# Experts of an attention and mixture-of-experts layer: plain scatters in place of adding scatters

## What is computed

```
x = x + cross_attention(layernorm(x), ctx)     # per token: 16 heads by 16 heads, softmax
n = layernorm(x)
shared = (silu(n @ sfc1.T) * (n @ sfc2.T)) @ sfc3.T
top_w, top_idx = top_k(n @ gate_w.T, 2);  top_w = softmax(top_w)
moe = sum over the 2 choices: top_w * ( silu(n @ w1[e].T) @ w2[e].T ),  e = top_idx
x = x + moe + shared
```

## Time and profile before

| | |
|---|---|
| median of 3 runs (lowest, highest) | 1812.68 us (1810.61, 1815.49) |
| the profiled execution, its own time | 1811.71 us |
| its span, first to last instruction | 1809.8 us |
| mean granted TensorE clock | 0.932 of full speed |
| PE, VectorE, ScalarE, GpSimd busy | 1490.7, 1250.5, 774.2, 1276.1 us |
| DMA bytes | 302.36 MB, mean 167 GB/s |

### The profile page before, as it was taken

One profiled execution on the slowest core, in us unless ns is written; L12 is line 12 of the kernel. 1 busy time (PEld: TensorE's weight loads), 2 busy tenths in 40 slices (PEclk: granted clock), 3 DMA queues, 4 the chain that ended last, 5 costly groups with the idle time before them and its releaser, 6 DMA issues.

```text
span 1809.8 us, 49252 instructions
## 1 busy us (share of the span) xinstructions
PE 1490.7 (82%) x17109; PEld 1315.5 (73%) x17110; DVE 1250.5 (69%) x3232; ACT 774.2 (43%) x1490; POOL 1276.1 (71%) x975
## 2 busy tenths in 40 slices
PE   5499999999999999999999999979776676676660
PEld 4477888888888888888888887758666665666650
DVE  7588888888888788888888887876434444334440
ACT  3244445445444444454455444425433333333330
POOL 5266666767676667666766766557888888888887
PEclk9699999999999999999999999999888889888885
DMA  8788888999898889888989988738777776777773
GB/s 195 136 212 184 171 174 209 197 178 192 209 183 179 192 194 188 180 192 211 180 174 210 201 174 185 178 137 213 136 130 134 134 133 108 132 132 134 134 113 36
DMA packets 929510, 302.36 MB, mean 167 GB/s; under 512 B 820882, under 2 KB 891160, under 8 KB 924480
## 3 DMA queue, kind: packets, MB, share of 16 engines
q1 hardware_dynamic: 859920, 178.50, 51.3%
q0 software_dynamic: 54432, 71.81, 21.7%
q10 hardware_dynamic: 15120, 51.57, 8.3%
HBM read 162.62 MB, written 143.43 MB: 169 GB/s over the span
## 4 chain that ended last, share of the span: by engine, by line
PE 38%; POOL 22%; issue 17%; DVE 14%; ACT 4%; SPq 2%; DMA 2%; POOLq 1%; DVEq 0%; ACTq 0%
POOL out L466 18%; ACT xn L568 3%; PE bank_a L1134 3%; PE bank_z L1119 3%; PE bank_y L1119 3%; PE bank_y L1121 3%; PE bank_y L1120 3%; PE bank_a L1273 3%; PE bank_z L1121 3%; PE bank_z L1120 3%; DVE ln_stats L879 2%; PE bank_a L1119 2%; PE bank_a L1121 2%; PE bank_a L1120 2%; PE bank_u L1119 2%
## 5 line engine op out<-in xcount | busy, mean ns | idle before, releaser
L466 POOL DMA_INDIRECT out<-v_area,tail x288 | 467.4, 1623 | 94.4 <-issue 89.1
L369 POOL DMA_INDIRECT slots<-xn,slot_i x256 | 263.8, 1031 | 134.5 <-DVE xn L830 71.7
L1119 PE MATMUL bank_y<-w_hi,xn_hi 128*128 x288 | 100.6, 349 | 148.8 <-DVE v_area L1075 81.7
L670 ACT ACTIVATE v_area<-bank_y,tail 128x256 f32<-128x256 f32 x144 | 60.5, 471 | 318.0 <-DVE tail L1067 314.1
L391 POOL TENSOR_TENSOR hid_lo<-hid,hid_hi 128x512 fp32r<-128x512 f32 x128 | 173.4, 1365 | 25.1 <-ACT hid_hi L539 23.6
L1119 PEld LDWEIGHTS bank_y<-w_hi,xn_hi 128*128 128x128 f32 x288 | 65.5, 228 | 163.9 <-issue 163.9
L1067 DVE COPY tail<-k_area 128x8 f32<-128x8 f32 x72 | 12.6, 175 | 245.7 <-DMA out<-v_area,tail 245.7
L539 ACT ACTIVATE hid_hi<-hid 128x512 fp32r<-128x512 f32 x128 | 80.6, 630 | 210.5 <-DVE hid L845 141.4
L1119 PE MATMUL bank_y<-wsh_out_hi,hid_hi 128*128 128x256 f32 x512 | 142.2, 278 | 0.0
L1120 PE MATMUL bank_y<-wsh_out_lo,hid_hi 128*128 128x256 f32 x512 | 141.9, 277 | 0.0
L1121 PE MATMUL bank_y<-wsh_out_hi,hid_lo 128*128 128x256 f32 x512 | 141.8, 277 | 0.0
(11 more groups left out here) (217 smaller groups left out, 4987.5 us busy)
## 6 DMA issues: line engine op xcount, KB each, us to landing
k_area<-slots SPq DMA_DIRECT2D x288, 129.0 KB
kv_dram<-w_sb SPq DMA_DIRECT2D x32, 1024.0 KB
x_sb<-in_x_in SPq DMA_DIRECT2D x32, 512.0 KB, 5.1
ctx_sb<-in_ctx_t SPq DMA_DIRECT2D x32, 512.0 KB, 5.0
q_dram<-q_sb SPq DMA_DIRECT2D x32, 512.0 KB
k_area<-kv_dram SPq DMA_DIRECT2D x256, 64.0 KB
w_sb<-q_dram SPq DMA_DIRECT2D x256, 64.0 KB
v_area<-kv_dram SPq DMA_DIRECT2D x256, 64.0 KB, 5.3
```

The lines of the kernel that those rows point to most:

```text
L369: pool.indirect_dma_start(slots[j], bass.IndirectOffsetOnAxis(ap=slot_i[:, j, i:i + 1], axis=0), row_of[j][:, i, :], None).then_inc(S[f"sc ...
L466: pool.indirect_dma_start(out, bass.IndirectOffsetOnAxis(ap=tail[:, r, t, 1 - j:2 - j].bitcast(u32), axis=0), y_ring[:, r, t, :], None, bo ...
L670: st = nc.scalar.activation(y_ring[:, r, t, :], Y[0][:, t * C:(t + 1) * C], ACT.Copy, scale=tail[:, r, t, j:j + 1])
L1119: mm(out, lhs_hi, rhs_hi, start=start, stop=False)
```

## The change

List 1, the second choices, is now worked first and list 0 second (`FIRST, SECOND = 1, 0`). A second pair of lists in DRAM, `sums1` and `sums0`, holds partial results at the same row numbers. In stage one GpSimd scatters base to the row of the token's second choice in `sums1`. A quad of list 1 loads these rows into `y_ring`, VectorE adds weight times expert row to them, and a plain indirect DMA passes the result on to the token's row of `sums0`, whose number now travels with the row. A quad of list 0 loads `sums0`, adds its part, and writes the token's row of `out`, also with a plain indirect DMA. Nothing is added in DRAM any more, and nothing is stored to `out` in stage one.

```diff
+FIRST, SECOND = 1, 0
+        sums = [nc.dram_tensor(f"sums{j}", [NO_TILE + P, C], f32).ap() for j in range(TOP)]
...
+        base = v_flat[:, 5120:5120 + BPC * C].rearrange("p (i f) -> p i f", i=BPC)
+        hid_of = [hid[:, 0, :], hid[:, 1, :]] + [x_ring_t[:, 2 * s:2 * s + 2, :].rearrange("p t f -> p (t f)") for s in range(2)]
...  # SP
+            def load_x(j, n, r, at_rows, first):
+                if not first:
+                    sp.wait_ge(S["tail_ready"], at(1, n - 4, 1))
+                    sp.sem_inc(S["slot_free"], 1)
+                for t in range(4):
+                    sp.dma_start(x_ring[:, r, t, :], slots[j][bass.ds(at_rows[t], P), :]).then_inc(S[f"loaded{r}"], 16)
+            def load_sums(j, n, r, at_rows, first):
+                if not first:
+                    sp.wait_ge(S[f"added{r}"], at(16, n - r, 0))
+                for t in range(4):
+                    sp.dma_start(y_ring[:, r, t, :], sums[j][bass.ds(at_rows[t], P), :]).then_inc(S[f"held{r}"], 16)
...
+            sp.wait_ge(S["padded1"], 2 * 16 * 3)
+            sp.wait_ge(S["scattered1"], 16 * BPC * CHUNKS)
+            first_rows = [tile_rows(q, q) for q in range(4)]
             for q in range(4):
-                load_quad(0, q, q, True, row_regs)
+                load_x(FIRST, q, q, first_rows[q], True)
+            sp.wait_ge(S["based"], 16 * BPC * CHUNKS)
+            sp.wait_ge(S["padded0"], 2 * 16 * 3)
+            for q in range(4):
+                load_sums(FIRST, q, q, first_rows[q], True)
             with sp.Fori(4, QUADS - 3, 4) as q:
                 for r in range(4):
-                    load_quad(0, q + r, r, False, row_regs)
+                    at_rows = tile_rows(q + r, r)
+                    load_x(FIRST, q + r, r, at_rows, False)
+                    load_sums(FIRST, q + r, r, at_rows, False)
...
+            for r in range(4):
+                load_x(SECOND, QUADS + r, r, second_rows[r], False)
+            for r in range(4):
+                sp.wait_ge(S[f"added{r}"], 16 * QUADS)
+            for r in range(4):
+                load_sums(SECOND, QUADS + r, r, second_rows[r], True)
...  # GpSimd, stage one
+            def scatter_base(c, par, tiles):
+                if tiles[0] == 0:
+                    pool.wait_ge(S["base_ready"], at(2, c, 2))
+                    pool.sem_inc(S["scatter_marked"], 1)
+                for i in tiles:
+                    pool.indirect_dma_start(sums[FIRST], bass.IndirectOffsetOnAxis(ap=slot_i[:, par, FIRST, i:i + 1], axis=0),
+                                            base[:, i, :], None).then_inc(S["based"], 16)
...  # GpSimd, stage two
-            def add(j, q, r):
-                n = j * QUADS + q
-                pool.wait_ge(S["ey_act"], at(1, n, 1))
-                pool.wait_ge(S["ey_dve"], at(1, n, 1))
-                pool.sem_inc(S["add_marked"], 1)
+            def pass_on(n, j, r):
+                target, last = (out, TOKENS - 1) if j == SECOND else (sums[SECOND], NO_TILE + P - 1)
                 for t in range(4):
-                    pool.indirect_dma_start(out, bass.IndirectOffsetOnAxis(ap=tail[:, r, t, 1 - j:2 - j].bitcast(u32), axis=0),
-                                            y_ring[:, r, t, :], None, bounds_check=TOKENS - 1, oob_is_err=False,
-                                            compute_op=ALU.add).then_inc(S[f"added{r}"], 16)
+                    if t % 2 == 0:
+                        pool.wait_ge(S["y_ready"], at(2, n, t // 2 + 1))
+                        pool.sem_inc(S["add_marked"], 1)
+                    pool.indirect_dma_start(target, bass.IndirectOffsetOnAxis(ap=tail[:, r, t, 1 - j:2 - j].bitcast(u32), axis=0),
+                                            y_ring[:, r, t, :], None, bounds_check=last, oob_is_err=False).then_inc(S[f"added{r}"], 16)
...  # ScalarE: store_base and expert_y go; x_round(c + 2) moves into turned_out, between its two pairs
...  # VectorE
-                if s >= 2:
-                    dve.wait_ge(S["hid_split"], at(SB, c, s - 1))
+                if not first:
+                    dve.wait_ge(S["hid_split"], at(SB, c - 1, s + 1))
...
+            def expert_y(n, j, r):
+                dve.wait_ge(S["tail_ready"], at(1, n, 1))
+                dve.wait_ge(S[f"held{r}"], at(16, n - r, 64))
+                for t in range(4):
+                    if t % 2 == 0:
+                        dve.wait_ge(S["ey_full"], at(2, n, t // 2 + 1))
+                    st = nc.vector.scalar_tensor_tensor(out=y_ring[:, r, t, :], in0=Y[t // 2][:, t % 2 * C:(t % 2 + 1) * C],
+                                                        scalar=tail[:, r, t, j:j + 1], in1=y_ring[:, r, t, :],
+                                                        op0=ALU.mult, op1=ALU.add)
+                    if t % 2:
+                        st.then_inc(S["y_ready"], 1)
```

More of the change, by code:

```diff
@@ L300, in _ @@
             chunk(CHUNKS - 1, False, True)
-            def load_quad(j, q, r, first, row_regs):
-                sp.reg_load(row_regs, slot_row[0:1, bass.ds((q + j * QUADS) * 4, 4)])
-                rows = [sp.snap(reg, min_val=0, max_val=NO_TILE) for reg in row_regs]
-                if not first:
-                    sp.wait_ge(S["tail_ready"], at(1, j * QUADS + q - 4, 1))
-                    sp.sem_inc(S["slot_free"], 1)
-                for t in range(4):
-                    sp.dma_start(x_ring[:, r, t, :], slots[j][bass.ds(rows[t], P), :]).then_inc(S[f"loaded{r}"], 16)
             sp.wait_ge(S["s_full"], 2 * CHUNKS)
@@ L321, in _, with tile_rows @@
                 sp.dma_start(slots[j][NO_TILE:NO_TILE + P, :], pad[:, 0, :]).then_inc(S["no_tile_stored"], 16)
-            row_regs = [sp.alloc_register(f"tile_row{t}") for t in range(4)]
+                sp.dma_start(sums[j][NO_TILE:NO_TILE + P, :], pad[:, 0, 0:C]).then_inc(S["no_tile_stored"], 16)
+            row_regs = [[sp.alloc_register(f"tile_row{r}_{t}") for t in range(4)] for r in range(4)]
+            def tile_rows(n, r):
+                sp.reg_load(row_regs[r], slot_row[0:1, bass.ds(n * 4, 4)])
+                return [sp.snap(reg, min_val=0, max_val=NO_TILE) for reg in row_regs[r]]
@@ L335, in _ @@
+            sp.wait_ge(S["scattered0"], 16 * BPC * CHUNKS)
+            second_rows = [tile_rows(QUADS + r, r) for r in range(4)]
+            for r in range(4):
[4 more added lines that the diff above has]
+                load_sums(SECOND, QUADS + r, r, second_rows[r], True)
+            with sp.Fori(QUADS + 4, TOP * QUADS - 3, 4) as q:
                 for r in range(4):
-                    load_quad(1, q + r, r, False, row_regs)
+                    at_rows = tile_rows(q + r, r)
+                    load_x(SECOND, q + r, r, at_rows, False)
+                    load_sums(SECOND, q + r, r, at_rows, False)
@@ L359, in ln2_power, with scatter @@
                 nc.gpsimd.tensor_tensor(ln2_shift[:, :], ln2_minus[:, :], ln2_rstd[:, :], ALU.mult).then_inc(S["ln2_shifted"], 1)
-            SCATTERS = [(j, i) for j in range(TOP) for i in range(BPC)]
-            def scatter(c, rows):
+            SCATTERS = [(j, i) for j in (FIRST, SECOND) for i in range(BPC)]
+            def scatter(c, par, rows):
                 if rows[0] == SCATTERS[0]:
@@ L449, in _ @@
             pool.wait_ge(S["pad_ready"], 1)
-            pads(0)
+            pads(1)
             hid_split(CHUNKS - 1, range(1, SB))
-            scatter(CHUNKS - 1, SCATTERS[BPC:])
+            scatter(CHUNKS - 1, 1, SCATTERS[BPC:])
+            scatter_base(CHUNKS - 1, 1, range(BPC))
             pool.wait_ge(S["w2_hi_ready"], 1)
@@ L606, in _ @@
             ln2(0, 0, True)
[L607 removed]
+            turned_out(0, True)
             def body(c, par, first, ahead, ahead_2):
[L610 to L613 removed]
+                exps(c, range(2))
                 gap_exps(c - 1)
@@ L661, in e_round, with quad @@
                 nc.scalar.activation(e_hi[:, par, :], e_hid[:, par, :], ACT.Copy).then_inc(S["e_hi_ready"], 1)
-            def expert_y(n, j, r, first):
-                act.wait_ge(S["ey_full"], at(2, n, 1))
-                act.wait_ge(S["tail_ready"], at(1, n, 1))
-                if not first:
-                    act.wait_ge(S[f"added{r}"], at(16, n - r, 0))
-                for t in range(2):
-                    st = nc.scalar.activation(y_ring[:, r, t, :], Y[0][:, t * C:(t + 1) * C], ACT.Copy, scale=tail[:, r, t, j:j + 1])
-                st.then_inc(S["ey_act"], 1)
-            def quad(n, j, r, before_this, last):
+            def quad(n, r, before_this, last):
                 expert_tanh(n, r % 2, before_this < 2)
@@ L887, in residual, with base_sum @@
                 nc.vector.tensor_scalar(ln2_minus[:, :], ln2_mv[:, :, 0], -1.0, None, ALU.mult).then_inc(S["ln2_mean"], 1)
-            def base_sum(c, par):
+            def base_sum(c, par, first):
                 for j in range(2):
                     dve.wait_ge(S["acc_full"], at(2, c, j + 1))
+                    if j == 0 and not first:
```

(3 more changed lines are left out.)

198 lines of the change are left out of this document (88 added, 110 removed).

## The result

The changed kernel took 1855.33 us (median of 4 runs, 1851.81 to 1858.49), the kernel before 1814.09 beside it: ratio 1.0221, 95% interval [1.0181, 1.0261]. It is slower by 41 us, about 2%; I had said 1730 us, some 82 us faster. The profiled run took 1852.70 us with a span of 1850.9.

A forecast was written before the change was run, and what follows sets the result against it. It took PE to bound stage one and GpSimd's making of adding DMAs stage two, 7.7 us a quad. 1261 - 9 + 35 P + 14.1 + 35 P + 15.6, with P = 6.4, gave 1730 us; 8-in-10 range 1670 to 1785.

The forecast's parts named there:

- So the additions fit: Stage one: GpSimd's idle time takes four more scatters a chunk, 5.2 us; the scatter of rows starts some 0.4 us later.
- -9 us: Stage one: VectorE no longer waits 0.68 for GpSimd; 0.3 of it counted over 30 chunks, bounds -20 and +45.
- the ring: Stage two: waits from multiply-add through scatters, landing and loads to the multiply-add three quads on, 19.3 us with lag.
- turning 1.09, half of down 0.7 and its end 0.2: 2.0: Last term of the ring: PE's work from the landed x rows to VectorE's next multiply-add, 2.0 us.
- P: Time per quad in stage two: 6.4 us, bounds 5.4 and 7.7, break-even at 7.57.
- rival 2: Stage two: the plain indirect DMA costs GpSimd as much as the adding one, 7.5 us a quad, 1807 us; chance 0.07.
- 0.8 of lag: Stage two: the last load lands 0.8 us late because loads and scatters share the 16 DMA engines.
- rival 1: Stage two: the ring is loose and the DMA engines set the pace at 5.4 us a quad, 1660 us; chance 0.17.
- rival 3: Stage two: both landings grow by 2.1 us on shared engines, P = 7.8, 1828 us; chance 0.06.
- The start of stage two: Base scatters, w2 split, pads and first `sums` loads precede the first multiply-add, at 1261 us; it was 1244.19.
- The turn of the lists: Between quads 35 and 36 all of list 1 must land before `sums0` is read: 14.1 us between their multiply-adds.
- Rival 4: Stage one: GpSimd, filled up, is late with scaling or hidden splits, 1.5 us a chunk, 1784 us; chance 0.12.

The follow-up runs named there:

- the third set: Later set of runs in which the changed kernel ran again word for word beside its variants: 1809.80 us, ratio 0.9942 to the kernel before.
- e3_plain: Kernel before with its stage-two scatters writing in place of adding: 1790.52 us, run again 1797.84 us.
- e8_both: Changed kernel with rounding and splitting of x in their old places and loads of x rows one quad ahead of loads of `sums`: 1732.97 us.
- e9_act_both: Changed kernel with rounding and splitting of x in their old places and loads of `sums` from ScalarE's queue: 1726.14 us.
- e2_no_sums: Changed kernel without the stage-two loads of `sums` after the first four quads of each list: 1862.18 us.
- e10_hid_later: Changed kernel with GpSimd's third split of hid behind one more scatter of x rows: 1824.12 us, run again 1828.01 us.
- e16_act_hid_third: Changed kernel with loads of `sums` on ScalarE's queue and the later split of hid, run a third time: 1669.88 us.

## Why the prediction was wrong

Three steps failed. In stage one it was "So the additions fit", and with it the -9 us: the last scaling came 21.0 us later than in the kernel before in the result, and 38.3 later in the third set. In the ring it was the term "turning 1.09, half of down 0.7 and its end 0.2: 2.0", which measures 3.3. And P had no term at all for the stops, 66 us in the result, whose cause stays open. The first two, with some 5 us more at the start and the end of stage two, would have made 1805 and not 1730; it took the third to make the change a loss.

Against the profiled run of the third set, 1804.85 us, the forecast (1729.7 before rounding) adds up as follows: 1729.7 + 47.3 (stage one: last scaling at 1209.2, not at 1161.9) + 3.9 (start) + 22.7 (from the first to the last indirect DMA 488.7, where I had 466.0) + 1.2 (end) = 1804.8. Against the run of the result: 1729.7 + 30.0 + 3.6 + 88.3 + 1.2 = 1852.8 (1852.70 measured).

- **What bounded stage two before**: the adding DMAs on GpSimd at 7.7 us a quad, which the trace and the changed kernel's GpSimd (49 of 100 us busy) bear out. That plain scatters alone would free it was not shown, since `e3_plain` met the stops both times.
- **Price of a plain scatter**, 1.0 us and 1.3 from start to start: measured at 1.00 and 1.29, so rival 2 is out. The multiply-add took 0.478 us, at the upper end of 0.34 to 0.48; I had taken 0.44.
- **The ring**, P = 6.4: the mechanism was right, shown by `e8_both` and `e9_act_both`, which break it in two ways and land at the same 5.8 us. The size was 0.3 us short a quad: 6.88 by a measure in which I had 6.56. Medians of its terms in the third set, from 1320 to 1540 us: from the multiply-add to GpSimd's first DMA 1.8 (1.84 forecast), the four DMAs 4.9 (4.9), to the first load of `sums` 2.8 (2.7), to the last load of x rows 4.4 (3.6), to the turning 3.1 (3.4, and 0.8 of lag), to the next multiply-add 3.3 (2.0). The sum is 20.3 and not 19.3, and the last term is the one that was too small, because its path isn't through down: in program order VectorE's multiply-add stands behind its split of the hidden values and its copy of the tail, and these wait for ScalarE, which first copies the turned rows. At one quad the turning starts at 1410.18 us, and then come:

```profile
1410.87 1.09 ACT L683 ACTIVATE k_area<-bank_a 128x512 f32<-128x512 f32 x2 [2.77 <-PE bank_a L1386]
1411.85 0.63 ACT L697 ACTIVATE xn_hi<-v_area 128x512 fp32r<-128x512 f32 x1
```

```profile
1412.51 0.69 DVE L1075 TENSOR_TENSOR xn_lo<-v_area,xn_hi 128x512 fp32r<-128x512 f32 x1 [2.97 <-ACT xn_hi L697]
1413.12 0.17 DVE L1088 COPY tail<-k_area 128x8 f32<-128x8 f32 x1
1413.43 1.66 DVE L1096 SCALAR_TENSOR_TENSOR v_area<-bank_y,tail,v_area 128x256 f32<-128x256 f32 x4
```

- **What the ring costs** is 1.1 us a quad, about 80 us; rival 1's 5.4 is close to the 5.8 that is left without it. The clock rises with it, from a granted 0.90 from 1300 to 1500 us in the third set's changed kernel to 1.00 from 1350 to 1500 us in `e9_act_both`; how much of the gain is clock isn't shown.
- **Lateness from the DMA engines**: rival 3 asked for P = 7.8 by longer landings, and the result has a quad of 7.81. Its number, not its cause: `e2_no_sums` halves the loads and keeps 7.86, and its DMA engines are busy 43% of 1350 to 1500 us.
- **The stops**, 0.93 us a quad or 66 us in the result, had no term and no rival. They alone turn a tie into a loss: in the third set the change is worth 0.6%.
- **The start of stage two**: I had 92.0 us from the last scaling to the first indirect DMA, it was 95.6 (75.2 before). The turn of the lists had 14.1 us; GpSimd's first DMA of quad 35 and that of quad 36 start 12.3 us apart (1558.11 and 1570.43).
- **Stage one**: the step that failed is "So the additions fit", and with it "so I count 0.3 of it, 30 chunks, -9 us". VectorE's wait for the hidden split did go. But I had asked whether GpSimd has room (it has: 163 of 200 us busy in the fastest kernel) and not what its instructions meet on VectorE. Two places tell. The first is new, and it is in the run of the result and in the third set alike. Three base scatters now stand ahead of the softmax scaling; it starts at 715.08 us, 1.0 us after VectorE has finished the inverse sums that it needs (714.05), and VectorE's small two-input sum beside it ends with it:

```profile
714.60 1.62 DVE L823 TENSOR_TENSOR hot_sum<-hot_sum,hot_new 128x32 bf16<-128x32 bf16 x1
```

```profile
715.08 1.07 POOL L438 TENSOR_TENSOR w_sb<-w_sb,row_inv 128x512 f32<-128x512 f32 x1
```

```profile
722.16 0.50 PE L1143 MATMUL bank_z<-xn_hi,w_lo 128*128 128x512 f32 x1 [0.68 <-DVE th L853]
```

That sum takes 0.64 us on the mean in the kernel before, 0.61 without the base scatters, 1.53 in the result and 1.62 in the third set. VectorE has no idle time from it to `th`, a step of the shared block, and PE waits for `th`: 10.2 us in 16 chunks in the third set, 2.9 in the result, with 8.0 more ahead of the same matmul for which that trace names no releaser, none before and none without the base scatters. No experiment moved this overlap by itself, and `e10_hid_later` and `e16_act_hid_third` still have the wait (9.4 and 10.0 us). The second place, `ctx_lo`, is older than the change: its halves take 1.41 us on the mean in the kernel before, 1.44 without the base scatters, 1.51 in the result and 1.47 in the third set. PE's wait there is 17.1 us in 16 chunks before (the earlier trace rows has one of 1.02), 18.0 without the base scatters and 17.5 in the result, so in the result it had not grown. In the third set it is 24.4, 1.10 and 1.84 in turn, the second with the low clock behind it, and stage one is 17 us longer there than in the result. Why it grew in that set and not in the other, with the same program, is open. Rival 4 had the right size, 1.5 us a chunk, and the late scaling; the cause it gave, GpSimd filled up, is half of the story.

What stays open is the stops. Shown is that they come and go between sets of runs with the same program on the same chip (1815, 1817 and 1670 us), that they strike all kernels with plain scatters of one set together, that the kernel before has none in stage two, and that each trace with them or from a set with them holds 23,000 to 27,500 semaphore events and each without them 39,000 to 41,000. Whether the missing records are part of the cause (something that the recording does to the engines) or another effect of it, I can't tell, and no run here tells why adding scatters are spared. The loading of instructions hardly explains them: from 1300 to 1700 us the run of the result has 11 instruction packets in 400 us, the kernel before 5. SyncE's moves of over 0.6 us go with the missing records: 22 to 53 of them from 1250 us on in the traces with stops, none anywhere in the seven traces of the sets without.

## What to carry to other kernels

When loads for two buffers stand in one queue, write down for each what it waits for, and put the one that waits for a landing last or in a queue of its own; here that was worth about 80 us. Before you fill an engine's idle time, look at which two-input work of VectorE its reading instructions will then run beside, what small instructions of VectorE they stretch, and what PE's pause costs in clock as well as in waiting. And run the kernel itself again in every set: a gain of 43 us between two sets was no gain at all.

## What the runs showed of the hardware

- Two subtractions side by side on VectorE and GpSimd: VectorE's took 1.47 us on the mean, up to 2.56, and 0.69 when moved apart by one scatter. A 128x32 sum on VectorE took 1.5 to 1.6 us beside GpSimd's softmax scaling, against 0.64 where the scaling began earlier.
- A pause of PE of 1.10 us left its matmuls 0.12 us apart; after one of 1.84 us the next 15 came 0.21 apart, at a granted clock of 0.50, the lower of its two levels (1.2 in place of 2.4 GHz).
- In some sets ScalarE stood still for up to 9.8 us in stage two with nothing in the trace to hold it, and SyncE's register moves took 0.70 us each in those moments in place of 0.03.
- An indirect DMA without an add cost GpSimd 1.00 us in all three new uses (base, list to list, output), against 1.62 with it.
